# Phase 1 of a spectral attention and expert kernel: two buffers for the spectrum, a transform in two halves, one tap on ScalarE, turned rows through another PSUM bank

## What is computed

```python
Xh = rfft(chunks, axis=2)                      # 33 frequencies per chunk of 64 rows
X_low, X_high = Xh[:, :, :4], Xh[:, :, 4:]
A_r, A_i = attention(X_low.real), attention(X_low.imag)   # 16 heads, 4 kv heads, causal by chunk
H = gelu(causal_conv(X_high, dw, 7 taps)) @ pw            # real and imaginary part each
g = sigmoid(chunks.mean(axis=2) @ gate_w.T)
Y = irfft(concat(alpha * A + (1 - alpha) * X_low, H * g + X_high))
x = layernorm(x + Y)
dist = sqrt(|x|^2 + |centroid|^2 - 2 x @ centroid.T)      # top 2 of 8, softmax of the two
x = layernorm(x + sum_e weight_e * (silu(x @ Wg[e] + bg[e]) * (x @ W1[e] + b1[e]) @ W2[e] + b2[e]))
```

## Time and profile before

| what | us |
|---|---|
| median of three runs | 563.54 |
| lowest, highest | 560.66, 565.66 |
| the profiled execution, its own time | 561.65 |
| its span in the profile | 559.8 |
| TensorE's matmuls busy | 502.2 |
| VectorE, ScalarE, GpSimd busy | 363.6, 349.8, 289.5 |

### The profile page before, as it was taken

One profiled execution on the slowest core, in us unless ns is written; L12 is line 12 of the kernel. 1 busy time (PEld: TensorE's weight loads), 2 busy tenths in 40 slices (PEclk: granted clock), 3 DMA queues, 4 the chain that ended last, 5 costly groups with the idle time before them and its releaser, 6 DMA issues.

```text
span 559.8 us, 13552 instructions
## 1 busy us (share of the span) xinstructions
PE 502.2 (90%) x3988; PEld 478.3 (85%) x3988; DVE 363.6 (65%) x1045; ACT 349.8 (62%) x746; POOL 289.5 (52%) x423
## 2 busy tenths in 40 slices
PE   4777989989989876999999999999999999999990
PEld 4665977977977665899999999999999999999980
DVE  3778798888888899733334465564646455666763
ACT  3465788788788567455555556566575756755551
POOL 0152545635635544454444446767676767654453
PEclk9879999999999965799999999999999999999996
DMA  8340164155253014110000001111111111100000
GB/s 225 123 125 15 51 170 128 55 154 132 64 142 108 2 46 53 25 27 17 22 16 22 16 22 26 36 35 36 35 36 36 36 35 35 35 21 16 21 30 28
DMA packets 47183, 31.56 MB, mean 56 GB/s; under 512 B 12123, under 2 KB 44710, under 8 KB 47126
## 3 DMA queue, kind: packets, MB, share of 16 engines
q1 hardware_dynamic: 42214, 21.77, 15.2%
q0 software_dynamic: 4096, 8.66, 5.7%
q10 hardware_dynamic: 816, 0.41, 0.3%
HBM read 22.13 MB, written 8.69 MB: 55 GB/s over the span
## 4 chain that ended last, share of the span: by engine, by line
PE 55%; DVE 4%; issue 1%; DMA 1%; ACT 1%; POOL 0%; DVEq 0%; ACTq 0%; POOLq 0%
PE ps L1657 26%; PE ps L1682 18%; PE ps L1672 9%; PE ps L1666 1%; DVE xT L1313 1%; DMA xs<-rows_dram,idx 1%; PE ps L1239 1%; POOL out_dram L1618 0%; DVE xs L1862 0%; ACT xs L1734 0%; DVEq L1587 0%; PE ps L1498 0%; ACT xT L1232 0%; DVE prod L1281 0%; DVE R L1287 0%
## 5 line engine op out<-in xcount | busy, mean ns | idle before, releaser
L1657 PE MATMUL ps<-wts,xh 128*128 x620 | 153.5, 330 | 0.1
L1847 DVE TENSOR_TENSOR h<-ps,sg 128x684 f32<-128x684 f32 x78 | 67.5, 866 | 82.9 <-PE ps L1657 75.1
L1635 POOL TENSOR_TENSOR xl<-xT,xh 127x128 fp32r<-127x128 f32 x155 | 68.0, 457 | 98.2 <-ACT xh L1751 92.2
L1682 PE MATMUL ps<-w2s,hT 115*128 (+1 forms) x930 | 116.5, 274 | 0.3 <-DVE xs L1862 0.3
L1682 PEld LDWEIGHTS ps<-w2s,hT 115*128 115x128 f32 (+1 forms) x930 | 109.9, 191 | 0.6 <-issue 0.6
L1657 PEld LDWEIGHTS ps<-wts,xh 128*128 128x128 f32 x620 | 103.9, 189 | 0.5 <-issue 0.3
L1764 ACT ACTIVATE sg<-ps 128x684 f32<-128x684 f32 x78 | 57.6, 739 | 67.2 <-PE ps L1657 67.2
L1657 PE MATMUL ps<-wts,xl 128*128 x310 | 99.1, 320 | 0.0
L1773 ACT ACTIVATE hT<-ps 114x768 f32<-114x768 f32 x78 | 62.9, 807 | 56.4 <-PE ps L1672 56.4
L1862 DVE SCALAR_TENSOR_TENSOR xs<-ps,xs 128x128 f32 x155 | 54.4, 351 | 54.9 <-PE ps L1682 37.7
L1618 POOL DMA_INDIRECT out_dram<-xs,idx x64 | 62.8, 982 | 25.8 <-issue 17.4
(11 more groups left out here) (291 smaller groups left out, 840.2 us busy)
## 6 DMA issues: line engine op xcount, KB each, us to landing
xt<-_attn_hidden_states_dram SPq DMA_DIRECT2D x8, 512.0 KB, 6.1
xres<-_attn_hidden_states_dram SPq DMA_DIRECT2D x7, 512.0 KB, 5.2
rows_dram<-x1s SPq DMA_DIRECT2D x7, 512.0 KB, 3.7
w2s<-in_L_ffn_W_dram SPq DMA_DIRECT2D x8, 171.0 KB
st<-in_L_ffn_Wg_dram SPq DMA_DIRECT2D x8, 171.0 KB, 2.3
st<-in_L_ffn_W_dram SPq DMA_DIRECT2D x8, 171.0 KB, 2.4
stl<-in_L_ffn_Wg_dram SPq DMA_DIRECT2D x8, 171.0 KB, 3.3
stl<-in_L_ffn_W_dram SPq DMA_DIRECT2D x8, 171.0 KB, 3.9
```

The lines of the kernel that those rows point to most:

```text
L1635: v.tensor_tensor(xl[0:D - 1, i % 2, u, :], xT[0:D - 1, bass.ds(off[u], P)], xh[0:D - 1, i % 2, u, :].bitcast(F32), ALU.subtract).then_inc ...
L1657: mm = pe.matmul(ps[:, 2 * w + u, 0:HF], a[:, t % 2, u, :], wflat[:, bass.ds(w1[u] + (b + w * HF), HF)], start=(k == 0), stop=(k == 2))
L1682: mm = pe.matmul(ps[:, low(t) + u, 0:D], hT[0:n, t % 2, u, k, :], w2flat[0:n, bass.ds(w1[2 + u] + k * D, D)], start=(k == 0), stop=(k == 2))
L1847: v.tensor_tensor(h[:, t % 2, 0:units(t), :], ps[:, 2:2 + units(t), 0:HF], sg[:, 0:units(t), :], ALU.mult).then_inc(s["h_done"], 1)
```

## The change

`XF` gets a second buffer, chosen by the parity of t, which is passed to every step as `par`. So that the parity is known in the code, the loop runs over pairs of steps: steps 0 to 3 are written out, and the loop makes two rounds of two steps. The transform of sequence t is cut in two: bank 0's four matmuls stand ahead of the transposed probabilities, bank 1's behind them, and ScalarE's two copies follow the same order. They wait for the taps of the sequence before the last one. The first tap of `YI` goes from VectorE to ScalarE, behind `VB`. The second half of the turned rows goes through bank 0, so its wait is gone, and their two copies on ScalarE stand behind both halves of the softmax. A one-element exponential into `spare` stands ahead of the copies of `Vs`, so that the table for the exponential is loaded there.

```diff
-        XF = sb("XF", [P, NC, C])
-        XR, XI = XF[:, :, 0:FR], XF[:, :, FR:C]
+        spare = sb("spare", [P, 1])
+        XF = sb("XF", [P, 2, NC, C])
...
-            step(2, True, True, True)
-            with eng.Fori(3, B) as s_:
-                step(s_, True, True, True)
+            step(2, True, True, True, 0)
+            step(3, True, True, True, 1)
+            with eng.Fori(2, B // 2) as s_:
+                step(2 * s_, True, True, True, 0)
+                step(2 * s_ + 1, True, True, True, 1)
             tail()
...
-            def transform(t, T):
+            def transform(t, T, halves):
...
-                for h in range(2):
+                for h in halves:
                     for j in range(4):
                         mm = pe.matmul(ps[:, h, j * P:(j + 1) * P], xt[:, 4 * h + j, :], fwd, start=True, stop=True)
                     mm.then_inc(s["dft_done"], 1)
...
                 def turned(h):
-                    pe.wait_ge(s["x1t_ev"], 2 * (t - 2) + h)
                     for j in range(4):
-                        mm = pe.transpose(ps[:, 7, j * P:(j + 1) * P], x1s[:, 4 * h + j, :], ident)
+                        mm = pe.transpose(ps[:, (7, 0)[h], j * P:(j + 1) * P], x1s[:, 4 * h + j, :], ident)
                     mm.then_inc(s["t_done"], 1)
-                if Y and not T:
-                    transform(t, T)
                 if Y:
+                    transform(t, T, range(0, 1))
...
-                if T:
-                    transform(t, T)
                 if Y:
+                    transform(t, T, range(1, 2))
...
-                    pe.wait_ge(s["x1t_ev"], 2 * (t - 1))
                     for j in range(TB):
+                        if j % 4 == 0:
+                            pe.wait_ge(s["x1t_ev"], 2 * (t - 2) + j // 4 + 1)
                         mm = pe.matmul(ps[:, 7, j * C:(j + 1) * C], x1T[:, j, :], cT[:, :], start=True, stop=True)
...
-            def spectrum(t):
-                for h in range(2):
-                    act.wait_ge(s["dft_done"], 2 * t + h + 1)
-                    act.wait_ge(s["conv_done"], 2 * t)
-                    nc.scalar.activation(XF[:, 8 * h:8 * h + 8, :]..., ps[:, h, :], ACT.Copy).then_inc(s["xr_ev"], 1)
+            def spectrum(t, T, par, h):
+                act.wait_ge(s["dft_done"], 2 * t + h + 1)
+                if T:
+                    act.wait_ge(s["conv_done"], 2 * (t - 1))
+                nc.scalar.activation(XF[:, par, 8 * h:8 * h + 8, :]..., ps[:, h, :], ACT.Copy).then_inc(s["xr_ev"], 1)
+            def first_tap(t, par, first):
+                act.wait_ge(s["xr_ev"], 2 * (t + 1))
+                if not first:
+                    act.wait_ge(s["gelu_done"], 2 * t)
+                nc.scalar.activation(YI[:, :, :], XF[:, par, :, FR + LOW - 1:C], ACT.Copy, scale=dw[:, 1, KS - 1:KS]).then_inc(s["tap_done"], 1)
...
+                    first_tap(t, par, not Y)
...
+                if X:
+                    act.wait_ge(s["prep_al"], 2)
+                    if Y:
+                        act.wait_ge(s["unread"], t)
+                    nc.scalar.activation(spare[:, :], al[:, :], ACT.Exp).then_inc(s["unread"], 1)
...
-                if X:
-                    softmax(0)
-                if T:
-                    turned(0)
-                if Y:
-                    for h in range(2):
+                for h in range(2):
+                    if Y:
                         act.wait_ge(s["vt_done"], 2 * (t - 1) + h + 1)
                         if T:
                             act.wait_ge(s["z_done"], 2 * (t - 1))
                         nc.scalar.activation(Vs[:, 4 * h:4 * h + 4, :]..., ps[:, 2 + h, :], ACT.Copy).then_inc(s["vs_ev"], 1)
+                    if X:
+                        softmax(h)
                 if T:
+                    turned(0)
                     turned(1)
-                if X:
-                    softmax(1)
...
                     else:
-                        dve.wait_ge(s["conv"], 14 * t + 7 * i + k)
+                        if i and k == 1:
+                            dve.wait_ge(s["tap_done"], t + 1)
+                        else:
+                            dve.wait_ge(s["conv"], 13 * t + 6 * i + k)
...
-                    conv(t, 1, not Y, range(0, 2))
+                    conv(t, par, 1, not Y, range(1, 2))
```

More of the change, by code:

```diff
@@ L339, in steps @@
         def steps(eng, step, tail):
[L341 to L345 removed]
+            step(0, True, False, False, 0)
+            step(1, True, True, False, 1)
+            step(2, True, True, True, 0)
[3 more added lines that the diff above has]
+                step(2 * s_ + 1, True, True, True, 1)
             tail()
@@ L360, in _, with step @@
             sp.dma_start(kvr[0:E, 7, :], g["cent"]).then_inc(s["raw3_in"], 16)
-            def step(t, X, Y, T):
+            def step(t, X, Y, T, par):
                 if X:
@@ L424, in _ @@
             pe.wait_ge(s["const_in"], 32)
-            transform(0, False)
+            transform(0, False, range(2))
             pe.wait_ge(s["raw_in"], 32)
@@ L678, in gelu @@
                     nc.scalar.activation(G[:, i, :, 0:2 * n], y[:, :, :].rearrange("p (j c) f -> p j (c f)", c=2), ACT.Gelu).then_inc(s["gelu_done"], 1)
-                if Y and not T:
-                    spectrum(t)
+                if Y:
+                    spectrum(t, T, par, 0)
                 if Y:
@@ L688, in step @@
                         nc.scalar.activation(PT[:, i, :, :].rearrange("p k m -> p (k m)"), ps[:, 2 + i, :], ACT.Copy).then_inc(s["pt_ev"], 1)
-                if T:
-                    spectrum(t)
                 if Y:
+                    spectrum(t, T, par, 1)
                     gelu(t - 1, 1, not T)
@@ L822, in settle, with conv @@
                 dve.wait_ge(s["prep_cst"], 7)
-            def conv(t, i, first, taps):
-                y, x, n, off = ((YR, XR, HR, LOW), (YI, XI, HI, LOW - 1))[i]
+            def conv(t, par, i, first, taps):
+                y, n, off = ((YR, HR, LOW), (YI, HI, FR + LOW - 1))[i]
                 for k in taps:
                     m = n - k
-                    src = x[:, :, off:off + m]
+                    src = XF[:, par, :, off:off + m]
                     w = dw[:, i, KS - 1 - k:KS - k]
@@ L879, in step @@
                 if X:
-                    conv(t, 0, not Y, range(KS))
+                    conv(t, par, 0, not Y, range(KS))
                 if Y:
@@ L918, in step @@
                     scores(0)
-                    conv(t, 1, not Y, range(2, 3))
+                    conv(t, par, 1, not Y, range(2, 3))
                     scores(1)
-                    conv(t, 1, not Y, range(3, 4))
+                    conv(t, par, 1, not Y, range(3, 4))
                 if X:
@@ L929, in step @@
                         if i == 0:
-                            conv(t, 1, not Y, range(4, 5))
+                            conv(t, par, 1, not Y, range(4, 5))
                 if Y:
@@ L940, in step @@
                 if X:
-                    conv(t, 1, not Y, range(5, KS))
+                    conv(t, par, 1, not Y, range(5, KS))
                 if Y:
```

17 lines of the change are left out of this document (8 added, 9 removed).

## The result

| | before | after |
|---|---|---|
| time, median of 20 runs each | 562.88 us (559.62 to 565.66) | 565.72 us (560.61 to 570.54) |
| ratio to before, 95% interval | | 1.0049 [1.0030, 1.0069] |
| profiled execution, its span | 561.65 us, 559.8 us | 566.33 us, 564.5 us |

The changed kernel is half a per cent slower: 2.8 us in the medians, 4.7 in the two profiled executions. Forecast were 564.3 us (560.5 to 568.5) and no difference above 1%; both held. Behind phase 1 nothing changed: from the transposed probabilities of the tail to the end of the span it is 559.8 - 184.30 = 375.5 us before and 564.5 - 189.92 = 374.6 after. So the whole loss lies where the prediction looked for it.

A forecast was written before the change was run, and what follows sets the result against it. TensorE bounds the round's first part, VectorE the second. Terms +3.3 +1.2 +1.0 -1.6 -5 x 0.90 +2 x 0.6 +3 x 0.05 gave +0.75, say +0.8 us: median 564.3 us, range 560.5 to 568.5.

The forecast's parts named there:

- +3.3 for the casts: Step 0: mask casts queue on VectorE behind the tap waiting for ScalarE, so TensorE's L519 starts 3.3 us later.
- +1.2 for the clock: Step 0: after the longer idle L519 and L523 may run at half clock, 0 to 2.3 us more, taken as +1.2.
- Step 1's second half, +1.0: Step 1: half the transform, formerly in TensorE's idle time, now stands behind L456 and costs 1.0 us.
- Step 2, -1.6: Step 2: the half transform that leaves had run slow, 3.17 / 2, so 1.6 us are gained.
- Steps 3 to 7, -5 x 0.90: Loop rounds: half the transform leaves the part where TensorE is the bound, gaining 0.90 us in each of five steps.
- The waits for xt, +2 x 0.6 + 3 x 0.05: Loop: the half transform meets xt's load earlier, costing 0.6 us in two steps and 0.05 in three.
- The discount: Loop: three of five xt loads, not behind a loop turn, go out 0.5 us earlier and are charged only 0.05.
- ScalarE's tap: Loop: the tap takes about 0.62 us within ScalarE's 0.55 us idle ahead of x1s; about nothing, 0.6 at most.
- rival (d): Loop: ScalarE's tap and dummy exponential delay x1s and so xt's load, +4.9 us in six steps, 569.2 us; chance 0.10.

The follow-up runs named there:

- casts' experiment: The changed kernel with VectorE's casts of mqb and mkb put ahead of the second tap of YI in step 0: 562.12 us, ratio 1.0010 to before.
- both edits: The changed kernel with step 0's mask casts ahead of the tap and xt's load issued behind the weight loads: 554.64 us, ratio 0.9883 to before.
- the tap back: The kernel with both edits, with the first tap of YI moved from ScalarE back to VectorE: 554.71 us, ratio 0.9862 to before.
- The experiment with the early load: The changed kernel with SyncE's steps written out and xt's load issued right behind the weight loads: 558.54 us, ratio 0.9943 to before.
- the control: The changed kernel with SyncE's steps written out and the order of its loads kept: 564.46 us, ratio 1.0058 to before.
- the transform in one piece: The kernel with both edits, transform whole again, in two versions: TensorE's matmuls alone moved, 565.50 us; ScalarE's spectrum copies also behind PT, 563.27 us.
- bank 7: The kernel with both edits, both turned rows through bank 7 again, ScalarE's copies and exponentials ordered as before: 554.94 us, ratio 0.9869 to before.

## Why the prediction was right, and where it was right by luck

The time lay in the range and the difference within 1%, but the sum behind them did not hold. One of its terms was off by 6.5 us, and another by 1.2 the other way. Up to the tail the sum said +0.8 us, and the table above has +5.62: 4.83 for the start, -0.16 and -2.01 for steps 1 and 2, +2.96 for steps 3 to 7, which were to bring -3.15.

**Steps 0 and 1, casts and clock: right.** Forecast were +3.3 for the casts and +1.2 for the clock. Measured are +3.33 and +1.89, less the 0.39 won ahead of L491, which is no work of the change: 4.83 late at the first L457. The casts' experiment gave it back. The clock term took 2.3 at most and counted on 1 us back from a shorter slow stretch at the first L457. About 0.6 came back in this trace, and it stands in step 1.

**Step 1's second half, +1.0: not met.** From step 1 to step 2 it is 22.49 us after and 22.65 before, no loss. TensorE ran at half clock there behind its idle time in both kernels. The half transform, 1.91 us, filled the wait of 0.23 us for PT, and the product with VB (L466) behind it found the full clock sooner: 2.41 us, where it took 3.75 before. But one execution is no proof. The same stretch takes 21.76 to 23.08 us in the seven traces with halves, 22.65 in the mean, and 21.76 to 22.65 in the five without, 22.32 in the mean. By these it costs about 0.3 us, with a spread from trace to trace that is larger than the term.

**Step 2, -1.6: 2.0 measured.** The mechanism was the one named; the rest of the transform too ran at full clock this time. That part is luck: in the kernels with both edits and with the tap back, step 2 had its half clock again (L459 1.94 us), and 1.04 us were gained.

**Steps 3 to 7, -5 x 0.90: right as a mechanism.** From L457 to mx it is 13.05 to 13.08 us where no half clock falls into it (13.10 forecast), and the round without the wait for xt is 20.4 to 20.56 with both edits. There the five steps are 4.75 us shorter than before (102.41 us from step 3 to the tail, 107.16 before), for 4.5 forecast.

**The waits for xt, +2 x 0.6 + 3 x 0.05: the step that failed.** They cost about 7.9 us. The rounds were to be 20.6 and 21.2 us and came at 21.85, 22.18, 23.26 and 22.40, and only the last at 20.43. The experiment with the early load shows it from the other side: from step 3 to the tail 110.12 us pass after, and 102.41 in the kernel with both edits. Three things were in it. The size: the load went out 1.1 to 1.9 us behind the end of x1s and took 6.1 to 7.0 us, not 6.0, against a TensorE that was ready 6.5 us behind mx. That is 1.10 to 1.37 us in three of the five steps (0.30 and 0.42 in the other two), where I had computed 0.7 to 0.8 and charged 0.6. The discount: I took the 0.53 us between L392 and L367 for the turn of the loop, and so priced three steps at next to nothing. But a step inside the loop's body has such gaps too (0.60 and 0.29 us here), and from the end of x1s to the issue it is 1.91 and 1.59 us there against 1.40 and 1.88 behind a turn:

```profile
114.14 0.42 SPq L390 DMA_DIRECT2D rows_dram<-x1s  x1
115.16 0.40 SPq L395 DMA_DIRECT2D xres<-_attn_hidden_states_dram  x1
115.85 0.72 SPq L370 DMA_DIRECT2D xt<-_attn_hidden_states_dram  x1
```

The steps that are written out are free of it, with 1.09 us in step 3 here and 1.08 in four of the control's five. So the cost was the loop's in all four of its steps, and not the turn's in two. And what I had left out: an idle time of this length can bring the lower clock with it. I had priced that in step 0, where I saw a long idle, and not in the loop, where the idle was my own forecast. The control's trace parts the two: with waits of 2.9 us and no half clock it takes 105.21 us from step 3 to the tail, 2.8 more than with the load early. Even without half clock the waits were thus worth twice their price.

**ScalarE's tap: right that it is harmless in the loop**, and rival (d) with it: x1s ends 0.76 us ahead of mx (110.76 + 3.18 = 113.94 against 114.70), as it did before (0.81). The dummy exponential was not tried apart.

So the forecast of 0.8 us over before met 4.7 in the profiled executions and 2.8 in the medians. That the time still lay in the range was luck, in two ways. The range had been stretched towards rival (d), a price for a late load of xt of nearly that size (+4.9 us), though by another mechanism: ScalarE did not delay the load, it was late as it stood. And the sum was set on a median of 563.54 from three runs, where twenty runs gave 562.88.

## What to carry to other kernels

Work that is moved forward into an idle time needs its data earlier by as much: follow its load back through the queue to what the issue waits behind, and move the issue with it (here 1.15%, more than the change itself had lost). When an operation goes to another engine, look at what is queued behind the instruction that now waits, in the first step above all: here two casts, which nothing tied to the tap, cost 3.3 us and a slow stretch. And test each part by itself: of the parts that were tried, the tap and the turned rows brought nothing that the time shows, and the halves all. The second buffer and the dummy exponential were not tried apart.

## What was not expected of the hardware

TensorE's clock fell behind quite short idle times, but not every time. In the rounds of steps 3 to 7, over the traces of the changed kernel and its variants, idle times of 0.77, 0.79, 0.81, 1.10, 1.36, 1.37 and 1.70 us were followed by 1.2 GHz, and each time about 1.7 us were lost. Others of 0.70, 0.87, 0.95, 0.97, 1.23 and, in the control with SyncE's steps written out, also 1.37 were not, and none up to 0.60 us was. The same 0.87 us ahead of the tail's transposes brought it in three kernels (casts first, and both with the transform in one piece) and not in the changed one. The 1.33 us ahead of the turned rows in the kernel before and in the one with bank 7 never brought it in the traces. What else decides is open. It would fit that the changed kernel's 20 runs spread over 9.9 us and the six of the kernel with both edits over 3.1, but this was not tried apart, and the kernel before spreads over 6.

The slow stretch behind the long idle time of step 1 did not grow with the work put into it, and it was not of one size either: it cost 2.8 us before, 2.25 in the changed kernel, 1.5 with the casts first and 2.9 with both edits.

The load of xt, 512 KB behind two other transfers of that size on the same queue, took 6.1 to 7.0 us in steps 3 to 7; issued behind the weights' loads instead it had a median of 5.7 over its eight issues. Sending it out sooner behind the same two did not always bring it sooner: in the control, step 4's load went out 1.08 us behind x1s instead of 1.40 and landed 8.56 us behind it instead of 8.42.
